# Two edits to an eight-core attention and FFN layer: a second set of buffers in the first layer norm, and one DMA issue moved from POOL to ACT

## What is computed

```python
x = x + layernorm(attn(layernorm(x)))      # layer norms without scale and shift
x = x + layernorm(ffn(layernorm(x)))
# attn: q, k, v = split(x @ qkv_w.T + qkv_b); for each offset o, head and position n
#   logit[o] = (q[n] . k[n-o]) / 8 * (1 + q[n] . scale_embed[o]) + pos_bias[o]
#   p = softmax over o; out[n] = sum over o of p[o] * v[n-o], times a gain of the head
#   attn = (out * sigmoid(x @ gate_w.T + gate_b)) @ out_w.T + out_b
# ffn: one complex 512 x 512 matrix, unfolded from two small tensors, on both halves of x
```

## Time and profile before

| | us |
|---|---|
| time before, median of two runs | 3219.0 (3209.83 and 3228.17) |
| profiled execution, whole | 3222.31 |
| its span on the slowest core (core 0), first to last instruction | 3220.8 |
| spans of the eight cores | 3191.8 to 3220.8 |
| chain that ended last: DMA, DVE, ACT, PE | 32%, 23%, 15%, 14% of the span |

### The profile page before, as it was taken

The page is one execution under the profiler, slowest core; times in us unless marked ns, Lnnn a source line. Parts: engine busy times, 40 slices in busy tenths (PEclk is TensorE's granted clock), DMA queues, the critical chain, the costliest instruction groups (busy, mean ns, idle before and its releaser), DMA issues.

```text
span 3220.8 us, 18351 instructions; the slowest of 8 cores (3191.8 to 3220.8 us)
## 1 busy us (share of the span) xinstructions
PE 803.8 (25%) x4872; PEld 377.9 (12%) x4872; DVE 1065.9 (33%) x1142; ACT 864.2 (27%) x952; POOL 348.5 (11%) x315
## 2 busy tenths in 40 slices
PE   0111786655651011111111110111111530001530
PEld 0000332212221000000000000000000210000210
DVE  1222001100002545445554444555445133223133
ACT  0222332211213332223333322333332132003333
POOL 1000000000000011112110122211013000210000
PEclk9999999976865555555555555555555765555765
DMA  2111211123322222222222223222222323002123
GB/s 60 52 53 52 27 17 10 21 54 56 59 70 100 70 48 58 62 60 61 62 60 48 58 61 56 60 64 60 53 58 55 79 94 122 5 5 66 33 87 122
DMA packets 396199, 184.99 MB, mean 57 GB/s; under 512 B 342880, under 2 KB 354160, under 8 KB 396096
## 3 DMA queue, kind: packets, MB, share of 16 engines
q1 hardware_dynamic: 147568, 82.54, 8.2%
q0 software_dynamic: 49744, 57.81, 8.1%
q10 hardware_dynamic: 198784, 43.46, 7.0%
HBM read 111.73 MB, written 78.32 MB: 59 GB/s over the span
## 4 chain that ended last, share of the span: by engine, by line
DMA 32%; DVE 23%; ACT 15%; PE 14%; issue 7%; ACTq 5%; SPq 1%; POOL 1%; DVEq 1%; POOLq 0%
PE kqps L318 8%; DVE rbuf L531 6%; DMA rimg<-rbuf 5%; ACTq L584 4%; ACT rbuf L532 4%; DMA xt<-xs 3%; DMA psp_img<-Pb 3%; DVE bandx L566 3%; DVE scr L563 3%; DMA qtok<-qts 2%; DMA accTb<-acch 2%; PE opps L750 2%; PE fps L897 2%; DMA q_img<-qtmp 2%; DMA ktok<-wcol 2%
## 5 line engine op out<-in xcount | busy, mean ns | idle before, releaser
L516 PE MATMUL genps<-kfm,qsl 64*128 64x160 f16 (+2 forms) x768 | 92.6, 338 | 1234.7 <-DMA qtb<-qtok 731.6
L318 PE MATMUL kqps<-y1fm,wcol 128*128 128x512 f16 x1408 | 372.5, 421 | 51.6 <-ACT qtmp L360 29.2
L531 DVE CAST rbuf<-genps 128x640 f16<-128x640 f32 (+2 forms) x96 | 331.7, 3456 | 139.8 <-DMA rimg<-rbuf 113.8
L532 ACT CAST rbuf<-genps 128x640 f16<-128x640 f32 (+2 forms) x96 | 331.8, 3456 | 152.5 <-DMA psp_img<-Pb 75.8
L516 PEld LDWEIGHTS genps<-kfm,qsl 64*128 64x128 f16 x768 | 40.4, 116 | 1300.8 <-issue 1300.6
L597 ACT ACTIVATE t2b<-t2b 128x736 f32<-128x736 f32 x16 | 13.1, 816 | 592.4 <-DVE t2b L594 592.4
L318 PEld LDWEIGHTS kqps<-y1fm,wcol 128*128 128x128 f16 x1408 | 144.1, 106 | 235.3 <-issue 119.4
L647 POOL DMA_DIRECT2D pspsb<-psp_img x48 | 25.3, 532 | 1136.6 <-DMA rimg<-rbuf 1030.9
L469 PE MATMUL pvps<-pspsb,vtok 128*64 128x128 f16 x384 | 111.9, 412 | 57.9 <-DMA pspsb<-psp_img 29.3
L482 DVE TENSOR_TENSOR outfl<-outfl,accTb 128x128 f16<-128x128 f16 x128 | 34.7, 271 | 276.7 <-DMA psp_img<-Pb 140.1
L351 DVE COPY vtok<-trpv 128x512 f16<-128x512 f16 x56 | 23.8, 425 | 271.8 <-PE trpv L345 271.8
(11 more groups left out here) (122 smaller groups left out, 1589.9 us busy)
## 6 DMA issues: line engine op xcount, KB each, us to landing
pspsb<-psp_img POOLq DMA_DIRECT2D x48, 512.0 KB, 5.4
x1r<-x_img ACTq DMA_DIRECT2D x32, 512.0 KB, 3.3
xt<-xs POOLq DMA_DIRECT2D x28, 512.0 KB, 3.8
rimg<-rbuf SPq DMA_DIRECT2D x32, 416.0 KB, 2.5
rimg<-rbuf SPq DMA_DIRECT2D x32, 384.0 KB, 2.5
rimg<-rbuf SPq DMA_DIRECT2D x32, 320.0 KB, 2.3
xres<-xs ACTq DMA_DIRECT2D x16, 512.0 KB, 3.5
x_img<-x1t SPq DMA_DIRECT2D x16, 512.0 KB, 2.6
```

What stands on the lines that cost most here:

```text
L318: e.matmul(_o, _s, _m, start=_st, stop=_sp),
L516: e.matmul(_o, _s, _m, start=True, stop=True, tile_position=_tp), waits, ("TS", 1))
L531: cpf = (lambda e, _o=pout, _i=pin: e.tensor_copy(_o, _i)) if eng == "vector" else \
L532: (lambda e, _o=pout, _i=pin: e.copy(_o, _i))
```

## The change

It has two parts. In the first layer norm, `xt`, `y1t` and the five small columns get a second copy, the tokens `ln_tok` and `tps_tok` are kept per copy, and the copy of tile tt-1 into `y1fm` is recorded after the transposes of tile tt. In stage B2, the three reads of `psp_img` are issued by ACT and counted on AQ. Line numbers after L234 shift by up to 7.

```diff
-        xt = [sb("xt0", [128, D], F32, e1a)] * 2
-        y1t = [sb("y1t0", [128, D], BF16, e1a)] * 2
-        sumc = sb("sumc", [128, 1], F32, e1a)
...
+        xt = [sb(f"xt{i}", [128, D], F32, e1a) for i in range(2)]
+        y1t = [sb(f"y1t{i}", [128, D], BF16, e1a) for i in range(2)]
+        sumc = [sb(f"sumc{i}", [128, 1], F32, e1a) for i in range(2)]
...
+        tps_all = {}
         for tt in range(NT):
             bs = tt % 2
             ld = S("gpsimd", lambda e, _o=xt[bs][:], _i=bass.AP(t["xs"], tt * 128 * D, [[D, 128], [1, D]]):
-                   e.dma_start(out=_o, in_=_i), (ln_tok[1],), ("GQ", 16))
+                   e.dma_start(out=_o, in_=_i), (ln_tok[bs],), ("GQ", 16))
...
-            ln_tok[1] = s3
+            ln_tok[bs] = s3
             tps = None
             for c in range(8):
                 tps = S("tensor", lambda e, _o=trp[bs][:, c * 128:(c + 1) * 128],
                         _i=y1t[bs][:, c * 128:(c + 1) * 128]:
                         e.transpose(_o, _i, idb[:]), (s3, ev_tok[bs], c2), ("TS", 1))
-            tps_tok[1] = tps
-            ev = S("vector", lambda e, _o=y1v[:, :, tt * 128:(tt + 1) * 128],
-                   _i=trp[bs][:].rearrange("p (c tq) -> p c tq", c=8):
-                   e.tensor_copy(_o, _i), (tps,), ("VS", 1))
-            ev_tok[bs] = ev
+            tps_tok[bs] = tps
+            tps_all[tt] = tps
+            if tt >= 1:
+                pb = (tt - 1) % 2
+                ev_tok[pb] = S("vector", lambda e, _o=y1v[:, :, (tt - 1) * 128: tt * 128],
+                               _i=trp[pb][:].rearrange("p (c tq) -> p c tq", c=8):
+                               e.tensor_copy(_o, _i), (tps_all[tt - 1],), ("VS", 1))
+        ev_tok[(NT - 1) % 2] = S("vector", lambda e, _o=y1v[:, :, (NT - 1) * 128: NT * 128],
...
-            rd = S("gpsimd", lambda e, _o=dst, _i=src: e.dma_start(out=_o, in_=_i),
-                   (psp_wr[qt], pv_tok.get((qt - 1, 7))), ("GQ", 16), batch=("pr", qt))
+            rd = S("scalar", lambda e, _o=dst, _i=src: e.dma_start(out=_o, in_=_i),
+                   (psp_wr[qt], pv_tok.get((qt - 1, 7))), ("AQ", 16), batch=("pr", qt))
```

More of the change, by code:

```diff
@@ L234, in build_program @@
     with contextlib.ExitStack() as e1a:
-        xt = [sb("xt0", [128, D], F32, e1a)] * 2
-        y1t = [sb("y1t0", [128, D], BF16, e1a)] * 2
-        sumc = sb("sumc", [128, 1], F32, e1a)
[L238 to L241, removed]
+        xt = [sb(f"xt{i}", [128, D], F32, e1a) for i in range(2)]
+        y1t = [sb(f"y1t{i}", [128, D], BF16, e1a) for i in range(2)]
+        sumc = [sb(f"sumc{i}", [128, 1], F32, e1a) for i in range(2)]
+        negm = [sb(f"negm{i}", [128, 1], F32, e1a) for i in range(2)]
+        ssq = [sb(f"ssq{i}", [128, 1], F32, e1a) for i in range(2)]
+        rstd = [sb(f"rstd{i}", [128, 1], F32, e1a) for i in range(2)]
+        nmr = [sb(f"nmr{i}", [128, 1], F32, e1a) for i in range(2)]
         trp = [psum(f"trp{i}", [128, 1024], BF16, e1a) for i in range(2)]
@@ L249, in build_program @@
             ld = S("gpsimd", lambda e, _o=xt[bs][:], _i=bass.AP(t["xs"], tt * 128 * D, [[D, 128], [1, D]]):
-                   e.dma_start(out=_o, in_=_i), (ln_tok[1],), ("GQ", 16))
[L251 to L258, removed]
-            ln_tok[1] = s3
+                   e.dma_start(out=_o, in_=_i), (ln_tok[bs],), ("GQ", 16))
+            v1 = S("vector", lambda e, _x=xt[bs][:], _o=sumc[bs][:]: e.tensor_reduce(_o, _x, mybir.AxisListType.X, ALU.add), (ld,), ("VS", 1))
+            v2 = S("vector", lambda e, _o=negm[bs][:], _i=sumc[bs][:]: e.tensor_scalar(_o, _i, -1.0 / D, None, ALU.mult), (v1,), ("VS", 1))
+            s1 = S("scalar", lambda e, _x=xt[bs][:], _y=y1t[bs][:], _b=negm[bs][:], _a=ssq[bs][:]:
+                   e.activation(_y, _x, AF.Square, bias=_b, scale=1.0, accum_out=_a), (v2, tps_tok[bs]), ("SS", 1))
+            s2a = S("scalar", lambda e, _o=rstd[bs][:], _i=ssq[bs][:]: e.activation(_o, _i, AF.Sqrt, bias=epsc[:], scale=1.0 / D), (s1,), ("SS", 1))
+            s2 = S("vector", lambda e, _r=rstd[bs][:]: e.reciprocal(_r, _r), (s2a,), ("VS", 1))
+            v3 = S("vector", lambda e, _o=nmr[bs][:], _m=negm[bs][:], _r=rstd[bs][:]: e.tensor_mul(_o, _m, _r), (s2,), ("VS", 1))
+            s3 = S("scalar", lambda e, _x=xt[bs][:], _y=y1t[bs][:], _b=nmr[bs][:], _r=rstd[bs][:]:
+                   e.activation(_y, _x, AF.Identity, bias=_b, scale=_r), (v3,), ("SS", 1))
+            ln_tok[bs] = s3
             tps = None
@@ L264, in build_program @@
                         e.transpose(_o, _i, idb[:]), (s3, ev_tok[bs], c2), ("TS", 1))
-            tps_tok[1] = tps
-            ev = S("vector", lambda e, _o=y1v[:, :, tt * 128:(tt + 1) * 128],
-                   _i=trp[bs][:].rearrange("p (c tq) -> p c tq", c=8):
-                   e.tensor_copy(_o, _i), (tps,), ("VS", 1))
-            ev_tok[bs] = ev
+            tps_tok[bs] = tps
[6 more added lines that the diff above has]
+        ev_tok[(NT - 1) % 2] = S("vector", lambda e, _o=y1v[:, :, (NT - 1) * 128: NT * 128],
+                                 _i=trp[(NT - 1) % 2][:].rearrange("p (c tq) -> p c tq", c=8):
+                                 e.tensor_copy(_o, _i), (tps_all[NT - 1],), ("VS", 1))
         sched.barrier()
```

## The result

The changed kernel takes 3047.4 us in the median of 11 runs (3039.9 to 3060.3), beside 3214.8 for the kernel before in 10 runs on the same chip. The ratio is 0.9484, with a 95% interval from 0.9458 to 0.951: 167 us less, where 161 were forecast.

What follows compares the result with a forecast made beforehand. The prediction took waits in chains, not full engines, to bound the first layer norm and attention rounds. From the profiled 3222.3 us it subtracted 135 (layer norm) and 26 (moved reads): 3061 us, range 3035 to 3100.

Steps and rivals of the forecast that it cites:

- The layer norm: First layer norm: doubled buffers and later copy cut the pace from 9.97 to 4.96 us a tile, saving 135 us.
- Buffers: First layer norm loop: a load waits for the last ACT operation two tiles earlier; 4.96 us a tile, the longest loop.
- DVE and ACT: First layer norm loop: square to `nmr`, copy of the tile before, next sum; 4.82 us a tile.
- queue: First layer norm loop: each load waits for the landing of the one before; at most 4.61 us a tile.
- the rival: First layer norm loads stretch to the slowest `wo_sb` landing, 6.3 us: pace 6.16, 103 us saved, 3093 us; chance 0.10.
- The move: Attention rounds: without three issues POOL starts 2.1 us earlier, gaining 1.6 us a round, 26 us in 16 rounds.
- its own wait for SQ is the one that the reads had: Attention rounds: POOL's first product waits for the same SQ count as the reads did, so it can start 2.1 us earlier.
- 15 to 35 us less attention: Test of the moved reads: if attention is not 15 to 35 us shorter than 1472 us, that term is wrong.
- a delay of the last POOL sum delays the round: Attention round's end: last POOL sum, transposing DMA, `band` reads and softmax follow one another, each waiting for the one before.
- The collision: Attention rounds: POOL's earlier start may block DVE `scr` products, losing 0 to 1.91 us a round; the skill's rule points towards 3 us saved.
- Costed at nothing: Reads on ACT cost nothing: 21.4 us of cover, less 1.6, before the first `band` read, against landings of at most 8.0.
- The sum: Whole kernel: 3222.3 - 135 - 26 = 3061 us, with nothing else moving.

Runs made afterwards that it cites:

- e4: Changed kernel with a third load buffer `xt` in the first layer norm; ratio 0.945 to the kernel before.
- e3: Changed kernel with the copy into `y1fm` back in its own tile, second buffers kept; ratio 0.9723 to the kernel before.
- e1: Kernel before with the layer norm edit alone, reads of `psp_img` left on POOL; ratio 0.9592 to the kernel before.
- e12: Kernel before, unchanged, run and profiled again; ratio 1.001 to the kernel before.
- e2: Kernel before with only the reads of `psp_img` moved to ACT, first layer norm as before; ratio 0.9879 to the kernel before.
- e7: Changed kernel, unchanged, run again on another chip; ratio 0.9436 to the kernel before.
- e8: Changed kernel with the six `band` reads waiting for exactly the round's writes of `rimg`, not all of SQ; ratio 0.8818 to the kernel before.
- e5: Changed kernel with the reads of `psp_img` issued by SP instead of ACT, PE waiting for exactly these; ratio 0.9716 to the kernel before.
- e9: Changed kernel with third load buffer and exact waits for far products, `band` reads and reads of `psp_img`; 2799.2 us, ratio 0.8717 to the kernel before.
- e10: Changed kernel with reads of `psp_img` on SP and far products waiting for exactly the writes of `rimg`; ratio 0.9403 to the kernel before.
- e11: Changed kernel with reads of `psp_img` back on POOL, recorded behind its products, ahead of the last sum; ratio 0.9483 to the kernel before.

## Why the prediction was right

**The layer norm.** The forecast was 135 us by a pace of 4.96; it was 132 by 5.07. Buffers, DVE and ACT, queue: e4 shows the first loop to be the one that rules and the second to be 4.81, and e3 shows what the copy's new place is worth. Of the 3 us that are missing, 6 x (5.28 - 4.96) = 1.9 lie in the first six steps, which still alternate between short and long (4.06 to 6.63 us), and 21 x 0.05 = 1.1 in the others. The loads did not stretch: they land in 3.9 us in the median and 4.7 at most, where the prediction took 3.9 and the rival 6.3.

**The move.** The forecast was 26 us, 1.6 a round. The start came 2.2 us earlier (scr to product 5.12 before, 2.88 after; 2.1 forecast), and 0.5 of it was lost again between the first product and the last sum: 1.73 a round, and 1.75 between the mean of the three executions with the reads ahead of POOL's products (before, e1, e12) and that of the five on ACT (after, e2, e3, e4, e7). The first round gave 4.6, since there the reads alone had held POOL back: the step "its own wait for SQ is the one that the reads had" is wrong for that round. With 14 inner rounds and 0.7 in the last it makes 4.6 + 24.5 + 0.7 = 30 us, so the term was sized too low by 4 us, 3 of them in the first round. e2's ratio, 29 to 49 us, allows that.

The attention stage as a whole fell by 39 us from before to after, by 37 from e1 to the mean of e2, e3 and e4, and by 26 from e12 to e7, each time on one chip. What differs is the issue time of the `band` reads: over 16 rounds it was 12 us shorter with the move in the first pair, 6 shorter in the second and 5 longer in the third. 30 + 12, 30 + 6 and 30 - 5 come within 3 us of the three. Since it went both ways, it can't be laid to the move.

The prediction named 15 to 35 us less attention as the test of this term, and the profiled executions differ by 39 in the mean of the cores and by 53 on the slowest, so by its own test the term fails. By rows 30 of the 39 are the move's; the `band` reads took 8.47 in the one and 7.75 in the other, and e12 had 7.41 without the move. The bound was set without the scatter of one execution.

That a delay of the last POOL sum delays the round, as the prediction has it, is true of this kernel only through the shared count: with the exact wait of e8 the softmax no longer waits for it.

**The collision.** The rule of the Trainium skill ("SBUF — State Buffer", section "Who interferes with whom") would, as the prediction reads it, have brought the move down towards 3 us. The exclusion is there: the `scr` product of 1346.12 began while L667 ran (until 1346.50) and ended 0.55 after it, L681 began within L672 and ended 1.08 after it. Here the operation that had started first did get through, unlike the one of 1308.01 in the earlier trace rows; the page speaks of the one that issues first, and a row gives only when an operation starts. But these products have reductions behind them with time to spare, and of the 2.2 us of earlier start 0.5 was lost, not all.

**ACT.** Costed at nothing, and nothing was paid: the reads land in 6.7 us at most, and the first `band` read still comes 4.2 us after the transposing DMA's issue, as in the earlier trace rows (1699.26 less 1695.03). e5 shows the price of the neighbouring choice that looks just as free.

**The sum.** 161 us were forecast, and the two medians differ by 167. The profiled execution was forecast at 3061 and took 3042.6, 18 less. In the means of the eight cores the layer norm saved 3 us less than forecast and attention 13 more: 4 because the move was sized too low, and the rest mostly the `band` reads of those two executions. Most of the other 8 us comes from comparing slowest cores: before, the slowest was 17 us over the mean of the eight, now 8.5. That the medians come within 6 us of the forecast is in part luck: the misses of the two terms, 3 us and 4 us, have opposite signs.

## What to carry to other kernels

Where a queue has one counted semaphore and a wait takes the count recorded so far, as here, a wait for one of its DMAs is a wait for all that were recorded before: ask of each wait who else is in the count. The change won 5% by double buffering and by moving three issues; one wait with the right count won another 6.5% (e8). The second buffers gave only half of what they could while the evacuation of a tile stood ahead of the next tile's first operation on an in-order engine (e3). A DMA's issuing engine is chosen by what stands behind it in that engine's list and by who waits for that queue (e5, e10, e11).

## What was not expected of the hardware

- Nearly twice the rate on eight cores cost the loads next to nothing: at 101 GB/s on a core they land in 3.9 us in the median and 4.7 at most, at 55 GB/s they landed in 3.8 and 4.7.
- The issue of the same six `band` reads on ACT took 7.4 to 8.8 us in the mean of an execution, with no edit to them, and 7.41 and 8.47 with the same kernel on two chips. It is the largest scatter in a round, and its cause stays open.
- DVE operations that meet a POOL operation ended 0.55 or 1.08 us behind it in the rows above, and 0.8 in e9: what a meeting cost there, 0.2 to 2.3 us, went by how long the POOL operation still had to run.
